# Last stage of a fused conv/attention kernel: image 3 first, own banks, taps of two pairs in turns

## Chip, cores and metric

The kernel runs on one core of one Trainium2 chip. The metric is the time of one execution on the device in microseconds (us), median of several runs. Inside a trace times are counted from the start of the profiled span.

## What is computed

The input x has 4 images of 128 channels and 16 x 16 points (N = 256 points). Four residual layers follow each other; each starts with a group norm `_gn` (32 groups of 4 channels, statistics per image):

```python
x = x + attention(_gn(x))        # L0: q, k, v projections, softmax(q k^T / sqrt(C)) v, output projection
x = x + binary_conv(_gn(x))      # L1: batch norm, sign, grouped 3x3 conv of signs, batch norm, residual, PReLU
x = x + depthwise_block(_gn(x))  # L2: 3x3 depthwise conv, norm, relu, prune, 1x1 conv, norm, relu, prune
x = x + linear_attention(_gn(x)) # L3: q,k,v; softmax(k) over points; context = k v^T per head; out = w_out (context q) + b
```

The change lies mostly in L2 and L3. In L2 a channel of the depthwise output is zeroed if its largest value is under 4.0, and a channel of the block's output if its largest value is under 0.001. L3 needs the group norm of x after L2 (x3), for each image by itself.

## The kernel before

Everything stays in on-chip memory; all loops are unrolled and the order of the work on every engine is a list of calls written out by hand. The engines are TensorE (PE), VectorE (DVE), ScalarE (ACT), GpSimd (POOL) and SyncE (SP, the output DMAs). Each takes its list strictly from top to bottom; a wait at one call holds back all calls below it on that engine. Semaphores tie the lists together.

**Depthwise convolution (L2), TensorE.** The images are worked in two pairs p = 0, 1. For each of the 9 taps, `depthwise(p, tap)` (L1499) issues 8 small fp32 matmuls: 4 blocks of 32 channels times 2 images, each on its own 32 x 32 tile of the array (`tile_of`, L1493). Each fp32 matmul is two passes in the trace, so a tap is 16 matmul records and 16 weight loads. The 8 tiles that pair 0 uses and the 8 that pair 1 uses are different ones, and the results lie in different banks. `less_mean(p)` (L1532) adds the norm's mean term as a tenth, equal step, and its end (`dw_mm`) lets ACT and DVE start on the pair: `relu1` (L702), `prune1_max` (L1160), `prune1_weights` (L1169). `group_means2(p)` (L1515) is a full-array matmul of statistics. `pointwise(p)` (L1552) is the 1 x 1 convolution; it waits for `relu1` and the pruned weights, first of r = 1, then of r = 0.

**x3 and its norm.** DVE reads the pointwise result: `prune2_max` (L1176), `prune2_floor` (L1182), `x3_out(b)` (L1190, gives x3 and its sum). ACT takes the squares, `square_sum3(b)` (L686). POOL corrects the sum, `x3_sum_less_floor(b)` (L492). `group_means3(b)` (L1544, matmul L1549) on TensorE waits for both. Then DVE `group_out(3, b)` and `group_var(3, b)` (L853, L860), POOL `gn_root` (L369) and DVE `norm3(b)` (L869; image 1 on POOL, L506) give the normalised image t3.

**L3, for each image b.** TensorE: `project_k3` (L1577), `project_v3` (L1596), `project_q3` (L1587). DVE `k3_max` (L1204), ACT `softmax3` (L708, exponentials e3 and their sum). TensorE `transpose_k` (L1608), ACT `kt3_out` (L722), TensorE `context` (L1622), DVE `context_out` (L1212), TensorE `project_context` (L1632), ACT `project_out` (L729, scaled by the inverse sum, which POOL's `rinv3_out`, L513, makes), TensorE `output` (L1642), DVE `x4_out` (L1218), output DMA (L329). Before the change all `project_context` results share bank 4, and `output(b)` uses banks 6 and 2 in turn, so `output(2)` waits for `x4_out(0)` and `output(3)` for `x4_out(1)`.

`keep_warm(n)` (L1337) issues n matmuls whose result nobody reads. `rinv3_out(b)` begins with this wait:

```python
def rinv3_out(b):
    pool.wait_ge(e3_ready, b + 1)      # the exponentials of image b
```

Of the kernel before, what the change touches and what calls it, by code (L numbers as in the profile page):

```python
# [20 lines left out]
N = H * W  # L21
# [30 lines left out]
def build(nc, x, early, late, out):  # L52
# [10 lines left out]
    with ctx:  # L63
# [153 lines left out]
        pj_ps = banks[4][:, 0:C]  # L217
        y_ps = [banks[(6, 2)[b % 2]][:, 0:N] for b in range(B)]
# [114 lines left out]
        def _(pool):  # L333
# [229 lines left out]
            norm3_second(1)  # L563
            out_bias_less_floor(2)
# [3 lines left out]
            rinv3_out(0)  # L568
            mean_with_floor(2)
            gn_root(3, 2)  # L570
            mean_with_floor(3)
            rinv3_out(1)
            gn_root(3, 3)
# [3 lines left out]
        def _(act):  # L577
# [147 lines left out]
            def project_out(b):  # L725
# [3 lines left out]
                nc.scalar.activation(proj[:, b, :], pj_ps, ACT.Copy,  # L729
# [41 lines left out]
            negative_part(1)  # L771
            negative_part(2)
            square_sum2(0)
            negative_part(3)
            square_sum2(1)
# [9 lines left out]
            softmax3(0)  # L785
            q3_out(0)
            kt3_out(0)
            square_sum3(2)
            square_sum3(3)
            softmax3(1)  # L790
            v3_out(1)
            kt3_out(1)
            project_out(0)
            q3_out(1)
            softmax3(2)
            v3_out(2)
            kt3_out(2)
            softmax3(3)
            project_out(1)
            v3_out(3)  # L800
            kt3_out(3)
            project_out(2)
            q3_out(3)
            project_out(3)
        @block.vector
        def _(dve):
# [217 lines left out]
            def bn1_mean():  # L1024
                dve.wait_ge(rstd_ready[1], B)
# [3 lines left out]
                settle("bn1_e2")  # L1029
                step(nc.vector.tensor_scalar(bn1_e2[:, 1:2], bn1_e2[:, 0:1], EPS, None, ALU.add),  # L1030
                     "bn1_e2_eps")

            def bn1_var():
                settle("bn1_e2_eps")
                mean = bn_mv[:, 0, 0:1]
# [227 lines left out]
            norm1(2)  # L1263
            bn1_mean()
            bn1_var()
            norm1(3)
# [14 lines left out]
            h1_out(2)  # L1281
            x2_first_out(0)
            x2_first_out(1)
            h1_out(3)
# [15 lines left out]
            x3_out(1)  # L1300
            group_out(3, 0)
            group_var(3, 0)
            prune1_max(1, 1)
            group_out(3, 1)
            norm3(0)
            group_var(3, 1)
            prune1_weights(1, 1)
            prune1_max(1, 0)
            prune1_weights(1, 0)
            k3_max(0)  # L1310
# [5 lines left out]
            x3_out(3)  # L1316
            k3_max(1)
            group_out(3, 2)
            group_var(3, 2)
            context_out(0)  # L1320
            group_out(3, 3)
            group_var(3, 3)
            norm3(2)
            norm3(3)
            k3_max(2)
            context_out(1)
            k3_max(3)
            q3_out(2)
            x4_out(0)
            context_out(2)  # L1330
            context_out(3)
            x4_out(1)
            x4_out(2)
            x4_out(3)
# [453 lines left out]
```

## Time and profile before

| what | value |
|---|---|
| median of 3 runs (lowest to highest) | 70.4 us (70.36 to 70.52) |
| the profiled execution's own time | 70.48 us |
| its span | 68.8 us |
| PE busy | 59.6 us (87%) |
| DVE / ACT / POOL busy | 43.2 / 33.7 / 32.8 us |
| granted TensorE clock | full in the whole span |

The span begins with the first and ends with the last recorded work; 1.7 us of the profiled time lie outside it. A busy share is an average over stages with different limits; which wait ends last must be read stage by stage.

### The profile page before, as it was taken

What the parts mean: (1) busy time and instruction counts of PE and PEld (TensorE: products, weight loads), DVE (VectorE), ACT (ScalarE), POOL (GpSimd) and SP (SyncE); (2) the same over time, 40 slices, a digit from 0 to 9 for tenths busy, and PEclk for the clock granted to TensorE, in tenths of its full rate; (3) what the DMA queues carried; (4) which work ended last, traced back from release to release, by engine and by line L of the source; (5) the groups of instructions that cost most, each with busy time, mean ns of one, the idle gap of its engine ahead of it and who ended that gap; (6) DMA issues with size and microseconds to landing.
All of it is one profiled execution on the core that took longest, in us unless ns stands there. A gap on an engine that the chain in (4) does not pass through costs nothing.

```text
span 68.8 us, 1882 instructions
## 1 busy us (share of the span) xinstructions
PE 59.6 (87%) x666; PEld 47.1 (68%) x666; DVE 43.2 (63%) x168; ACT 33.7 (49%) x106; POOL 32.8 (48%) x98
## 2 busy tenths in 40 slices
PE   3994998999999979299988999999999978999530
PEld 2772777989999858188855676665676966997310
DVE  3959868577755988864569900939395975443520
ACT  5202686496987220573177820603464775481500
POOL 5805385889997454970030062074657396330000
PEclk9999999999999999999999999999999999999999
DMA  0597220000000000000000000000000000002222
GB/s 0 147 404 233 41 39 2 0 0 0 0 5 0 14 0 0 0 5 10 0 0 0 0 0 10 0 10 0 0 0 0 10 0 5 0 0 76 74 79 76
DMA packets 2777, 2.13 MB, mean 31 GB/s; under 512 B 976, under 2 KB 2512, under 8 KB 2768
## 3 DMA queue, kind: packets, MB, share of 16 engines
q1 hardware_dynamic: 2768, 2.01, 9.6%
q8 instruction: 5, 0.08, 0.5%
q14 instruction: 4, 0.03, 0.2%
HBM read 1.49 MB, written 0.52 MB: 29 GB/s over the span
## 4 chain that ended last, share of the span: by engine, by line
PE 66%; DVE 10%; issue 10%; DMA 5%; POOL 2%; ACT 1%; SPq 1%
PE bank L1511 13%; PE bank L1466 6%; PE bank L1424 5%; DMA x<-in_x 5%; PE bank L1453 4%; PE bank L1577 3%; PE bank L1642 3%; PE bank L1563 3%; PE bank L1400 3%; PE bank L1596 3%; PE bank L1435 3%; PE bank L1587 3%; PE bank L1622 3%; PE bank L1393 3%; PE bank L1412 2%
## 5 line engine op out<-in xcount | busy, mean ns | idle before, releaser
L1340 PE MATMUL bank<-warm 128*128 128x256 bf16 x70 | 10.5, 304 | 1.2 <-POOL warm L353 1.2
L369 POOL TENSOR_TENSOR gn_rstd<-gn_var_eps,minus_half 128x1 f32<-128x1 f32 (+2 forms) x12 | 7.3, 610 | 5.6 <-DVE gn_var_eps L860 4.1
L1511 PE MATMUL bank<-x,dw_diag 32*32 32x256 f32 x288 | 9.2, 377 | 0.3 <-DVE x L1123 0.3
L1340 PEld LDWEIGHTS bank<-warm 128*128 128x128 bf16 x70 | 7.6, 114 | 2.6 <-POOL warm L353 1.1
L1511 PEld LDWEIGHTS bank<-x,dw_diag 32*32 32x32 f32 x288 | 5.2, 103 | 2.3 <-issue 0.9
L1466 PE MATMUL bank<-signs,conv_blocks 128*128 128x256 bf16 x36 | 4.3, 276 | 1.3 <-ACT signs L647 1.3
L1466 PEld LDWEIGHTS bank<-signs,conv_blocks 128*128 128x128 bf16 x36 | 3.4, 97 | 2.2 <-issue 1.6
L473 POOL TENSOR_TENSOR mean_diag<-ident_tile,gn_group 128x64 f32<-128x64 f32 x2 | 0.6, 294 | 8.1 <-DVE gn_group L1143 8.1
L1424 PE MATMUL bank<-k,q 128*128 128x256 f32 x16 | 4.2, 386 | 0.2 <-DVE k L953 0.2
L702 ACT ACTIVATE h<-bank,l_shift,dw_scale 128x256 f32<-128x256 f32 x4 | 2.3, 565 | 4.2 <-PE bank L1539 3.9
L1160 DVE TENSOR_SCALAR_CACHE_REDUCE h_linear<-bank,dw_scale 128x256 f32<-128x256 f32 x4 | 1.9, 480 | 3.8 <-PE bank L1539 3.8
L1453 PE MATMUL bank<-vt,probT 128*128 128x128 f32 x32 | 4.3, 277 | 0.0
L620 ACT ACTIVATE prob<-bank,nmax 128x256 f32<-128x256 f32 x8 | 3.7, 472 | 0.9 <-DVE nmax L958 0.9
L1453 PEld LDWEIGHTS bank<-vt,probT 128*128 128x128 f32 x32 | 4.0, 192 | 0.0
L647 ACT ACTIVATE signs<-res,bn_shift,bn_scale 128x256 bf16<-128x256 f32 x4 | 2.1, 592 | 3.7 <-issue 3.7
L686 ACT ACTIVATE squares<-x,floor 128x256 f32<-128x256 f32 x4 | 2.0, 508 | 3.5 <-DVE x L1190 3.4
L958 DVE TENSOR_REDUCE nmax<-bank 128x2 f32<-128x512 f32 x4 | 2.8, 692 | 1.4 <-PE bank L1424 1.3
L513 POOL TENSOR_TENSOR rinv<-sum,minus_one 128x1 f32<-128x1 f32 x4 | 2.2, 554 | 2.7 <-ACT e L708 2.7
L1642 PE MATMUL bank<-q,proj 128*128 128x256 f32 x8 | 2.5, 398 | 1.0 <-issue 1.0
L403 POOL TENSOR_TENSOR conv_blocks<-conv_sign,conv_mask 128x128 bf16<-128x128 bf16 x9 | 3.4, 401 | 0.1
L369 POOL TENSOR_TENSOR bn_rstd<-bn_var_eps,minus_half 128x1 f32<-128x1 f32 x2 | 1.2, 604 | 4.4 <-DVE bn_var_eps L1080 3.6
L1424 PEld LDWEIGHTS bank<-k,q 128*128 128x128 f32 x16 | 2.9, 196 | 0.6 <-issue 0.4
(197 smaller groups left out, 156.2 us busy)
## 6 DMA issues: line engine op xcount, KB each, us to landing
out<-x SPq DMA_DIRECT2D x4, 128.0 KB, 1.7
late_params<-in_late SPq DMA_DIRECT2D x1, 404.5 KB, 4.5
x<-in_x SPq DMA_DIRECT2D x1, 384.0 KB, 3.6
early_params<-in_early SPq DMA_DIRECT2D x1, 258.0 KB, 3.8
x<-in_x SPq DMA_DIRECT2D x1, 128.0 KB, 2.1
pw_weights<-in_late SPq DMA_DIRECT2D x2, 64.0 KB, 3.5
pw_weights<-in_late SPq DMA_DIRECT2D x4, 32.0 KB, 1.8
l_params<-in_late SPq DMA_DIRECT2D x4, 2.2 KB, 1.7
```

The source lines that it names most:

```text
L369: return nc.gpsimd.tensor_tensor(out_ap, in_ap, minus_half[:, 0:n], ALU.pow)
L403: ins = nc.gpsimd.tensor_tensor(conv_w[:, tap, :].rearrange("p (g o) -> p g o", o=CONV_GROUP), conv_sign[:, tap, :].unsqueeze(1).to_broadc ...
L513: nc.gpsimd.tensor_tensor(rinv3[:, b:b + 1], sum3[:, b:b + 1], minus_one[:, :], ALU.pow).then_inc(rinv3_ready, 1)
L620: nc.scalar.activation(prob[:, b, par, :], s_ps[b % 2][:, par * N:(par + 1) * N], ACT.Exp, bias=nmax[:, b, par:par + 1], accum_out=psum_ro ...
L702: nc.scalar.activation(h2[:, p, r, :], dw_ps[p][r], ACT.Relu, bias=l2_shift[:, 3 * p + r:3 * p + r + 1], scale=dw_scale[:, p, r:r + 1]).th ...
L958: nc.vector.tensor_reduce(nmax[:, b, :], s_ps[b % 2][:, :].rearrange("p (a c) -> p a c", a=2), X_AXIS, ALU.max, negate=True).then_inc(nmax ...
L1340: nc.tensor.matmul(bank[:, 0:N], warm[:, 0:C], warm[:, :], start=True, stop=True)
L1424: ins = nc.tensor.matmul(s_ps[b % 2][:, par * N:(par + 1) * N], q[:, b, par:N:2], k[:, b, :], start=True, stop=True)
L1453: ins = nc.tensor.matmul(o_ps[b][:, par * C:(par + 1) * C], probT[:, b, j, par, :], vt[:, b, j, :], start=(j == 0), stop=(j == 1))
L1466: ins = nc.tensor.matmul(conv_ps[b], conv_w[:, tap, :], signs[:, b, dy:dy + H, dx:dx + W], start=(tap == 0), stop=(tap == TAPS - 1))
L1511: nc.tensor.matmul(tile_of(p, i, r), dw_diag[of, tap, :], xs[2][of, 2 * p + i, dy:dy + H, dx:dx + W], start=(tap == 0), stop=False)
L1642: nc.tensor.matmul(y_ps[b], proj[:, b, :], q3[:, b, :], start=True, stop=True).then_inc(y3_mm, 1)
```

## The change

Three kinds of edits. (1) `project_context(3)` gets bank 5, `output(2)` bank 1 and `output(3)` bank 3, with the waits that go with them; `q3_out(3)` moves from ACT to DVE. (2) Taps 6, 7, 8 of pair 0 and 0, 1, 2 of pair 1 are issued in turns. (3) The calls of the last stage, and a few of the batch norms, stand in another order on all four engines. On POOL `rinv3_out(0)` now stands ahead of `out_bias_less_floor(2)` and `x3_sum_less_floor(2)`; on ACT `softmax3(0)` stands behind `square_sum3(3)` and `kt3_out(0)` ahead of `softmax3(1)`; on DVE `k3_max(0)` stands behind `x3_out(3)`, and `context_out(0)` between `norm3(2)` and `norm3(3)`; on TensorE `transpose_k(0)`, `context(0)` and `transpose_k(1)` stand behind `group_means3(3)` and ahead of `project_k3(2)`. `keep_warm(4)` comes in ahead of `group_means3(1)`.

```diff
--- before.py
+++ after.py
@@ -214,8 +214,8 @@
         k3_ps = [banks[(6, 2)[b % 2]][:, 0:N] for b in range(B)]
         vt_ps = banks[5][:, 0:N]
         kt_ps = banks[1][:, 0:N]
-        pj_ps = banks[4][:, 0:C]
-        y_ps = [banks[(6, 2)[b % 2]][:, 0:N] for b in range(B)]
+        pj_ps = [banks[i][:, 0:C] for i in (4, 4, 4, 5)]
+        y_ps = [banks[i][:, 0:N] for i in (6, 2, 1, 3)]
         gn_ps = banks[7]
         cx_ps = [banks[(3, 7)[b % 2]][:, 0:C] for b in range(B)]
 
@@ -561,16 +561,16 @@
             mean_with_floor(1)
             gn_root(3, 1)
             norm3_second(1)
+            rinv3_out(0)
             out_bias_less_floor(2)
             x3_sum_less_floor(2)
             out_bias_less_floor(3)
             x3_sum_less_floor(3)
-            rinv3_out(0)
             mean_with_floor(2)
             gn_root(3, 2)
             mean_with_floor(3)
+            gn_root(3, 3)
             rinv3_out(1)
-            gn_root(3, 3)
             rinv3_out(2)
             rinv3_out(3)
         @block.scalar
@@ -726,7 +726,7 @@
 
                 act.wait_ge(pj_mm, b + 1)
                 act.wait_ge(rinv3_ready, b + 1)
-                nc.scalar.activation(proj[:, b, :], pj_ps, ACT.Copy,
+                nc.scalar.activation(proj[:, b, :], pj_ps[b], ACT.Copy,
                                      scale=rinv3[:, b:b + 1]).then_inc(pj_ready, 1)
 
             act.wait_ge(setup_done, 1)
@@ -769,10 +769,10 @@
             bn2_diagonal()
             negative_part(0)
             negative_part(1)
+            square_sum2(0)
             negative_part(2)
-            square_sum2(0)
+            square_sum2(1)
             negative_part(3)
-            square_sum2(1)
             square_sum2(2)
             square_sum2(3)
             relu1(0, 0)
@@ -782,25 +782,24 @@
             relu1(1, 0)
             relu1(1, 1)
             v3_out(0)
-            softmax3(0)
             q3_out(0)
-            kt3_out(0)
             square_sum3(2)
             square_sum3(3)
+            softmax3(0)
+            kt3_out(0)
             softmax3(1)
             v3_out(1)
             kt3_out(1)
-            project_out(0)
             q3_out(1)
             softmax3(2)
             v3_out(2)
+            softmax3(3)
+            project_out(0)
             kt3_out(2)
-            softmax3(3)
-            project_out(1)
             v3_out(3)
             kt3_out(3)
+            project_out(1)
             project_out(2)
-            q3_out(3)
             project_out(3)
         @block.vector
         def _(dve):
@@ -1022,16 +1021,17 @@
                     op0=ALU.mult, op1=ALU.mult, accum_out=bn1_e2[:, 0:1]), "bn1_e2")
 
             def bn1_mean():
+                settle("bn1_e2")
+                step(nc.vector.tensor_scalar(bn1_e2[:, 1:2], bn1_e2[:, 0:1], EPS, None, ALU.add),
+                     "bn1_e2_eps")
                 dve.wait_ge(rstd_ready[1], B)
                 step(nc.vector.scalar_tensor_tensor(
                     out=bn1_tmp[:, 1, :], in0=bn1_dev[:, :], scalar=1.0 / B, in1=rstd[:, 1, :],
                     op0=ALU.mult, op1=ALU.mult, accum_out=bn_mv[:, 0, 0:1]), "bn_mv", 0)
-                settle("bn1_e2")
-                step(nc.vector.tensor_scalar(bn1_e2[:, 1:2], bn1_e2[:, 0:1], EPS, None, ALU.add),
-                     "bn1_e2_eps")
 
             def bn1_var():
                 settle("bn1_e2_eps")
+                settle("bn_mv", 0)
                 mean = bn_mv[:, 0, 0:1]
                 nc.vector.scalar_tensor_tensor(
                     out=bn_ve[:, 0:1], in0=mean, scalar=mean, in1=bn1_e2[:, 1:2], op0=ALU.mult,
@@ -1260,9 +1260,9 @@
             group_out(1, 3)
             group_var(1, 3)
             bn1_mean_sq()
-            norm1(2)
             bn1_mean()
             bn1_var()
+            norm1(2)
             norm1(3)
             bn_scale_out(0)
             bn_shift_out(0)
@@ -1278,9 +1278,9 @@
             h1_minus_out(0)
             h1_minus_out(1)
             bn2_minus_shift()
-            h1_out(2)
             x2_first_out(0)
             x2_first_out(1)
+            h1_out(2)
             h1_out(3)
             x1_h1_out(2)
             x1_h1_out(3)
@@ -1298,37 +1298,38 @@
             x3_out(0)
             prune2_floor(1)
             x3_out(1)
+            prune1_max(1, 1)
             group_out(3, 0)
             group_var(3, 0)
-            prune1_max(1, 1)
-            group_out(3, 1)
-            norm3(0)
-            group_var(3, 1)
             prune1_weights(1, 1)
             prune1_max(1, 0)
+            group_out(3, 1)
+            group_var(3, 1)
             prune1_weights(1, 0)
-            k3_max(0)
+            norm3(0)
             prune2_max(2)
             prune2_floor(2)
             prune2_max(3)
             x3_out(2)
             prune2_floor(3)
             x3_out(3)
+            k3_max(0)
             k3_max(1)
             group_out(3, 2)
             group_var(3, 2)
-            context_out(0)
             group_out(3, 3)
             group_var(3, 3)
             norm3(2)
+            context_out(0)
             norm3(3)
             k3_max(2)
+            k3_max(3)
             context_out(1)
-            k3_max(3)
             q3_out(2)
             x4_out(0)
             context_out(2)
             context_out(3)
+            q3_out(3)
             x4_out(1)
             x4_out(2)
             x4_out(3)
@@ -1627,9 +1628,11 @@
                 pe.wait_ge(cx_ready, b + 1)
                 if b == 0:
                     pe.wait_ge(x3_ready, B)
+                elif b < 3:
+                    pe.wait_ge(pj_ready, b)
                 else:
-                    pe.wait_ge(pj_ready, b)
-                nc.tensor.matmul(pj_ps, ctxT[:, b, :], lp[:, LC["woutT"]],
+                    pe.wait_ge(vt3_ready, B)
+                nc.tensor.matmul(pj_ps[b], ctxT[:, b, :], lp[:, LC["woutT"]],
                                  start=True, stop=True).then_inc(pj_mm, 1)
 
             def output(b):
@@ -1637,8 +1640,10 @@
                 pe.wait_ge(pj_ready, b + 1)
                 if b < 2:
                     pe.wait_ge(e3_ready, b + 3)
+                elif b == 2:
+                    pe.wait_ge(kt3_ready, B)
                 else:
-                    pe.wait_ge(x4_ready, b - 1)
+                    pe.wait_ge(cx_ready, 3)
                 nc.tensor.matmul(y_ps[b], proj[:, b, :], q3[:, b, :],
                                  start=True, stop=True).then_inc(y3_mm, 1)
 
@@ -1702,54 +1707,55 @@
             depthwise(0, 4)
             depthwise(0, 5)
             depthwise(0, 6)
+            depthwise(1, 0)
             depthwise(0, 7)
+            depthwise(1, 1)
             depthwise(0, 8)
+            depthwise(1, 2)
             less_mean(0)
-            depthwise(1, 0)
             group_means2(1)
-            depthwise(1, 1)
-            depthwise(1, 2)
-            pointwise(0)
             depthwise(1, 3)
             depthwise(1, 4)
+            pointwise(0)
             depthwise(1, 5)
             depthwise(1, 6)
             depthwise(1, 7)
-            group_means3(0)
             depthwise(1, 8)
             less_mean(1)
+            group_means3(0)
+            keep_warm(4, gap_warm_ps)
             group_means3(1)
             keep_warm(7, gap_warm_ps)
+            pointwise(1)
             project_v3(0)
             project_k3(0)
-            pointwise(1)
             project_q3(0)
-            transpose_k(0)
             project_k3(1)
             project_v3(1)
             project_q3(1)
-            context(0)
             group_means3(2)
             group_means3(3)
-            project_context(0)
+            transpose_k(0)
+            context(0)
             transpose_k(1)
             project_k3(2)
             project_v3(2)
             project_k3(3)
             context(1)
+            project_context(0)
+            transpose_k(2)
             project_q3(2)
-            transpose_k(2)
+            project_v3(3)
+            transpose_k(3)
+            project_context(1)
             output(0)
-            project_v3(3)
-            project_context(1)
-            transpose_k(3)
             context(2)
+            context(3)
             project_q3(3)
+            project_context(2)
+            project_context(3)
             output(1)
-            context(3)
-            project_context(2)
             output(2)
-            project_context(3)
             output(3)
```

## Rows read from the trace of the kernel before

**Rows 1.** The page's chain that ended last, share of the span by engine.
```profile
PE 66%; DVE 10%; issue 10%; DMA 5%; POOL 2%; ACT 1%; SPq 1%
```

**Rows 2.** Timeline, batch norm and first taps: start us, length us, engine, line, operation, count.
```profile
26.18 0.41 DVE L869 TENSOR_SCALAR res<-x,gn_group,gn_rstd 128x256 f32<-128x256 f32 x1
...
36.90 0.47 DVE L1123 SCALAR_TENSOR_TENSOR x<-h_neg,one_minus_a,bank 128x256 f32<-128x256 f32 x1
...
37.53 1.53 PE L1511 MATMUL bank<-x,dw_diag 32*32 32x256 f32 x48 [0.33 <-DVE x L1123]
```

**Rows 3.** Timeline of TensorE (PE matmuls, PEld weight loads), end of pair 0's taps to pointwise.
```profile
41.82 0.64 PE L1511 MATMUL bank<-x,dw_diag 32*32 32x256 f32 x16
...
42.25 0.42 PE L1539 MATMUL bank<-valid_sum,mean_diag 32*32 32x256 f32 x8
...
42.44 0.23 PEld L1511 LDWEIGHTS bank<-x,dw_diag 32*32 32x32 f32 x14
42.44 0.42 PE L1511 MATMUL bank<-x,dw_diag 32*32 32x256 f32 x3
42.47 0.38 PE L1539 MATMUL bank<-valid_sum,mean_diag 32*32 32x256 f32 x2
...
43.09 0.38 PE L1521 MATMUL bank<-gn_mean_sq,group_sum 128*128 128x2 f32 x2
...
44.76 1.14 PE L1563 MATMUL bank<-h,pw_kept 64*128 64x256 f32 x8
```

**Rows 4.** Timeline, from the last step of pair 1 to the last x3.
```profile
48.91 0.64 PE L1539 MATMUL bank<-valid_sum,mean_diag 32*32 32x256 f32 x16
...
51.70 1.13 PE L1563 MATMUL bank<-h,pw_kept 64*128 64x256 f32 x8
...
54.44 0.48 DVE L1190 SCALAR_TENSOR_TENSOR x<-bank,floor,x 128x256 f32<-128x256 f32 x1
```

**Rows 5.** Timeline, norm of x3 and start of the last stage's second half.
```profile
52.26 0.47 ACT L708 ACTIVATE e<-bank,nmax 128x256 f32<-128x256 f32 x1 [0.51 <-DVE nmax L1204]
52.64 0.19 ACT L708 ACTIVATION_READ_ACCUMULATOR e<-bank,nmax 128x1 f32 x1
...
54.31 0.51 ACT L686 ACTIVATE squares<-x,floor 128x256 f32<-128x256 f32 x1 [0.16 <-DVE x L1190]
54.38 0.27 POOL L492 TENSOR_SCALAR gn_mean_sq<-floor,x_sum 128x1 f32<-128x1 f32 x1 [0.56 <-DVE x L1190]
...
55.27 0.56 POOL L513 TENSOR_TENSOR rinv<-sum,minus_one 128x1 f32<-128x1 f32 x1
55.27 0.28 PE L1549 MATMUL bank<-gn_mean_sq,group_sum 128*128 128x2 f32 x2
...
56.61 0.38 PE L1608 MATMUL bank<-ident,e 128*128 128x128 f32 x2
...
57.02 0.38 ACT L722 ACTIVATE kt<-bank 128x256 f32<-128x256 f32 x1 [0.72 <-PE bank L1608]
...
57.16 0.70 PE L1577 MATMUL bank<-t,late_params 128*128 128x256 f32 x2 [0.17 <-DVE t L869]
```

**Rows 6.** Timeline, the end of the kernel.
```profile
62.71 0.61 PE L1622 MATMUL bank<-kt,vt 128*128 128x128 f32 x4
...
66.15 0.48 DVE L1218 SCALAR_TENSOR_TENSOR x<-bank,out_bias,x 128x256 f32<-128x256 f32 x1 [0.91 <-PE bank L1642]
```

**Rows 7.** The chain of waits in order of time: start us, length us, what.
```profile
59.48 0.43 PE bank L1587 x2
59.91 0.22 PE bank L1608 x2
...
63.54 0.50 issue
```

**Rows 8.** Timeline of TensorE's warm matmuls (L1340), at the start and later.
```profile
1.15 3.17 PE L1340 MATMUL bank<-warm 128*128 128x256 bf16 x14 [1.15 <-POOL warm L353]
...
49.72 0.92 PE L1340 MATMUL bank<-warm 128*128 128x256 bf16 x7
```

## The prediction

> **What bounds the kernel now.** I read the page's chain first: two thirds of what ended last is TensorE [rows 1]. So the order of TensorE's list matters most, but a third of the chain is short work of other engines that TensorE waits for. The timeline then shows where. From the first tap (37.53) to the second pointwise product (51.70) TensorE is nearly always occupied [rows 2 to 4]. Then it waits for the norm of x3: the statistics matmul of image 2 runs at 55.27, and the first k projection that needs its norm at 57.16 [rows 5]. From there to the last context product at 62.71 it is full again [rows 5, 6], and the last microseconds are turn-taking between TensorE, ACT and DVE, with 0.50 us "issue" ahead of an output product [rows 7]. A change of about 0.2%, or 0.14 us, is the least that a measurement of this kernel can tell from none.
>
> I go along the timeline; "at" means the start of an operation on the clock of the trace of before, and every shift is against it.
>
> **Step 1, batch norm and first taps.** `norm1(2)`, 0.41 us, no longer stands ahead of the batch-norm variance [rows 2]. The short products in front still take their time, so I take -0.17 us, between 0 and -0.41. `h1_out(2)` no longer stands ahead of the two `x2_first_out`; the second (36.90) also waits for the linear matmuls, so I take another -0.10 (0 to -0.40). The delayed `h1_out(2)` makes `square_sum2(1)` no later, since ACT had `negative_part(2)` ahead of it before too. First tap: 37.53 becomes 37.26 [rows 2].
>
> **Step 2, taps in turns.** Tap 8 of pair 0 starts at 41.82 and `less_mean(0)`, the next step on the same tiles, at 42.25: 0.43 us a step, while one step lasts 0.64 us from first start to last end [rows 3]. A tile takes a new pass each 0.22 us and each step has two, so a single pair is bound by its tiles. Pair 1 uses the other tiles. The one place where both are in flight is `less_mean(0)` with tap 0 of pair 1: the tap's first matmuls start at 42.44, 0.19 us behind 42.25, and ahead of the second pass of `less_mean(0)` at 42.47. So the pairs do overlap. But 14 of the tap's 16 weight loads begin only at 42.44, when tap 8, two steps back, is finishing (41.82 + 0.64 = 42.46) [rows 3]. I read this as a limit: a step can be taken up only when the step two before it retires. In turns that means 0.64 us for each two steps, where tiles alone would need 0.43 and no overlap 0.86.
> Pair 0's tap 6 was at 40.96 (41.82 - 2 x 0.43) and is now at 40.69. Three turns of 0.64 put `less_mean(0)` at 40.69 + 1.91 = 42.60, +0.35 against 42.25; its passes are stretched too, so its end and `group_means2(1)` come at 43.24, +0.15 against 43.09, with two more taps of pair 1 done. Between `group_means2(1)` and `pointwise(0)` stand two taps as before, 1.67 us (43.09 to 44.76) [rows 3]: `pointwise(0)` at 44.91, +0.15. The pruned weights, +0.4, are needed only for its second half, and are in time.
>
> **Step 3, to the second pointwise.** After `pointwise(0)` (1.07 us to the next step, its 1.14 [rows 3] less the overlap at its end) stand four taps instead of six and no statistics matmul among them: 44.91 + 1.07 + 4 x 0.44 = 47.73 for `less_mean(1)`, -1.18 against 48.91 [rows 4]. The warm matmuls began 0.81 us after it (49.72), seven lasting 0.92 us [rows 8]. The four new ones cost 0.5 us of TensorE at most and are covered: `group_means3(1)` waits till about 49.2 for DVE, which has `prune1_max(1, 1)` ahead of `group_out(3, 0)`. Then about 0.24 us for it (an estimate, a third of those 0.81) and 0.92 for seven warm ones give `pointwise(1)` at 50.41, -1.29 against 51.70 [rows 4]. It no longer waits behind `project_v3(0)` and `project_k3(0)`. The last x3 starts at 53.15 instead of 54.44 and ends at 53.64 [rows 4]. So far this is a gain of 1.29 us.
>
> **Step 4, what POOL waits for.** Here it is lost. `x3_sum_less_floor(2)` ran at 54.38 as soon as x3 was there, and `rinv3_out(0)` at 55.27 behind it [rows 5]. Now it stands behind `rinv3_out(0)`, which waits for `softmax3(0)`, which on ACT stands behind `square_sum3(3)`, which waits for the last x3. ACT squares images 2 and 3 in 0.51 us each, from 53.47 to 54.49. `softmax3(0)` takes 0.57 us to its read sum (52.26 to 52.64 + 0.19): 55.06. Then POOL: 0.07 us to notice, 0.56 for the reciprocal, 0.17 for a bias, 0.27 for the sum [rows 5]: 56.13. `group_means3(2)` at 56.23, +0.96 against 55.27 [rows 5]. The queue alone costs 1.29 + 0.96 = 2.25 us. Late with it: both x3 sums, both norms, and on TensorE all that stands behind.
>
> **Step 5, to the k projection of image 2.** Before, it came when its norm did. Now `transpose_k(0)`, `context(0)` and `transpose_k(1)` stand ahead. `group_means3(3)` is 0.7 us behind `group_means3(2)` (56.93), and 0.21 us later comes `transpose_k(0)` (57.14). Its copy on ACT starts some 0.43 us later and lasts 0.38 (56.61, 57.02) [rows 5]: done at 57.96. Only then ACT comes to `softmax3(1)`, 0.57 us, 58.53, for which `transpose_k(1)` waits: 58.63. One transpose is 0.22 us of TensorE [rows 7]: `project_k3(2)` at 58.85, +1.69 against 57.16 [rows 5]. Its norm, at about 58.15, is no longer what it waits for.
>
> **Step 6, to the last context product.** Before, 5.55 us (57.16 to 62.71) [rows 5, 6]. Now eight steps of 0.43 to 0.44 us (k, v of 2, k of 3, context 1, q of 2, v of 3, output 0, context 2), four of 0.22 (two `project_context`, two transposes) [rows 7], and about 0.27 us ahead of `transpose_k(3)`, since ACT has `softmax3(3)` and `project_out(0)` ahead of `kt3_out(2)`: 3.48 + 0.88 + 0.27 = 4.63 us, `context(3)` at 63.48. That is -0.92.
>
> **Step 7, the end.** Before, 3.44 us from `context(3)` to the last `x4_out` (62.71 to 66.15) [rows 6]. Now TensorE has `context(3)`, `project_q3(3)`, two `project_context`, and outputs 1, 2, 3 one behind the other: 0.44 + 0.43 + 2 x 0.22 + 2 x 0.44 = 2.19 to the start of `output(3)`, and some 0.66 to DVE, 2.85 us. The own banks are what allows this; the projection of image 3 is ready 0.1 us ahead of its turn. -0.59. `q3_out(3)` on DVE has its place in the wait for output 1: nothing; if DVE were late there, 0.4 us. The last three DMAs come 0.43 us apart instead of 1.3; nothing is taken for this (up to +0.1).
>
> **Sum.** +1.69 - 0.92 - 0.59 = +0.18 us at the last `x4_out`. The profiled execution took 70.48 us, so 70.66; the median is 0.08 lower, so 70.6.
>
> **Rivals.**
> - *A, the pairs overlap fully* (tiles alone, 0.43 us a turn). Then `less_mean(0)` is at 41.98, the product behind it 0.69 us earlier than in my sum, and all that follows TensorE with it: 69.9. For it: the tiles are separate. Against: the 14 late loads [rows 3]. The sum is 0.18 us over before and there are three turns, so at 0.58 us a turn it breaks even, and below 0.53 it is faster by over 0.2%. This case ends on the other side. 0.2.
> - *B, no overlap* (a turn costs 0.86). `group_means2(1)` comes 0.61 us later than in my sum: 71.2. Against: 42.44 before 42.47 [rows 3]. 0.08.
> - *C, the clock.* From about 54.2 to 58.2 TensorE has four tiny statistics matmuls and two or three small steps, a far emptier stretch than any before, where the full clock was kept. The first 14 warm matmuls took 3.17 us, 0.23 each, against 0.13 later [rows 8]: that is the price of the lower level, 1.2 instead of 2.4 GHz. If the clock falls near 58, some 3 us of TensorE's steps take nearly twice their time, of which waits hide half: 72.1. 0.12.
> - *D, the waits of step 4 and 5 are shorter*, as when the copy and softmax chain of images 0 and 1 is hidden and `project_k3(2)` comes at its norm, 58.15: 69.9. 0.1. That the order has no such queueing at all is excluded by the lists.
>
> On B: the Trainium skill, "TensorE: Matmul & The Clock Gate", section on packing small matmuls, says that matmuls are "strict FIFO, no reordering" in start and end. By that rule the pairs would hold each other up as in B, at 71.2. The records at 42.44 and 42.47 speak against it, and the measurement decides. On C: the same page's part on the clock gate says that the clock is gated down when TensorE has been idle; by it the time would be C's. No run here shows it inside a kernel.
>
> **How the numbers follow.** My sum 0.5, A 0.2, B 0.08, C 0.12, D 0.1. The sum's own range, from steps 1 and 5 to 7, is 70.2 to 71.1, a fifth of it within 0.2% of 70.4 or just below. The range must take in A and D on one side and B on the other, and leaves out C: 69.6 to 71.4. Faster: A, D and 0.02 = 0.32. Same: 0.18. Slower: the rest of the sum, B and C = 0.50.
>
> **What would show it.** Right: `less_mean(0)` about 0.64 us per turn behind tap 6 of pair 0; `pointwise(1)` at about 50.4; POOL's reciprocal of image 0 ahead of `x3_sum_less_floor(2)`, waiting for ACT; TensorE empty from about 54.2 to 56.2; outputs 1 to 3 back to back. Wrong: turns of 0.45 us or 0.86 us; `group_means3(2)` ahead of 55.5; a granted clock under full between 55 and 62; `project_k3(2)` ahead of 58.2.

## The result, and the profile of the changed kernel

The changed kernel is slower: ratio to before 1.044, 95% interval 1.038 to 1.050. Its four runs took 73.35, 73.65, 74.95 and 75.19 us, against 70.36 to 70.52 us for three of before and 71.99 for a fourth. Run again (below) it gave 71.78 to 73.55 us; the three lowest of those six have a ratio of 1.020 (1.017 to 1.022). The forecast was 70.6 us in a range to 71.4: the direction was right, the size was not, and the time lies outside the range.

TensorE has two clock levels, 2.4 and 1.2 GHz; the granted clock is the share of the full one that the profile reports, over a whole run or a stretch of it. A run of this kernel can hold a stretch at the lower level, early or late, so the mean granted clock is given where it matters. Single runs of all these kernels, of before too, can come out 1.5 us or more longer, and each ratio is of the runs near the lowest alone.

The timeline of the changed kernel (lines after 1340 are numbered one higher, after 1635 five higher), at the places of [rows 2 to 6]; start us, length us, engine, line, operation, count, and in brackets what ended the idle time before it:

```profile
38.88 1.53 PE L1512 MATMUL bank<-x,dw_diag 32*32 32x256 f32 x48 [0.31 <-DVE x L1123]
...
44.83 0.38 PE L1522 MATMUL bank<-gn_mean_sq,group_sum 128*128 128x2 f32 x2
...
46.51 1.14 PE L1564 MATMUL bank<-h,pw_kept 64*128 64x256 f32 x8
...
51.87 1.16 PE L1564 MATMUL bank<-h,pw_kept 64*128 64x256 f32 x8
...
54.62 0.48 DVE L1190 SCALAR_TENSOR_TENSOR x<-bank,floor,x 128x256 f32<-128x256 f32 x1
...
55.35 0.49 ACT L686 ACTIVATE squares<-x,floor 128x256 f32<-128x256 f32 x1
...
55.85 0.45 ACT L708 ACTIVATE e<-bank,nmax 128x256 f32<-128x256 f32 x1
...
56.47 0.56 POOL L513 TENSOR_TENSOR rinv<-sum,minus_one 128x1 f32<-128x1 f32 x1 [2.46 <-ACT e L708]
...
57.17 0.27 POOL L492 TENSOR_SCALAR gn_mean_sq<-floor,x_sum 128x1 f32<-128x1 f32 x1
...
57.53 0.35 PE L1550 MATMUL bank<-gn_mean_sq,group_sum 128*128 128x2 f32 x2 [1.68 <-issue]
...
58.90 0.38 ACT L722 ACTIVATE kt<-bank 128x256 f32<-128x256 f32 x1 [2.51 <-PE bank L1609]
...
59.34 1.22 PE L1623 MATMUL bank<-kt,vt 128*128 128x128 f32 x4 [0.47 <-ACT kt L722]
...
60.78 1.06 PE L1578 MATMUL bank<-t,late_params 128*128 128x256 f32 x2
...
65.57 1.05 PE L1623 MATMUL bank<-kt,vt 128*128 128x128 f32 x8
```

The queue of step 4 stands there as it was worked out: POOL idle for 2.46 us until the exponentials of image 0, the reciprocal, and behind it the sum of x3 (57.17) that TensorE waits for. What the sum did not hold is seen in lengths: a context product of 0.61 us [rows 6] (0.71 where it follows a wait, as in the run with the gap filled below) takes 1.22 us at 59.34, a k projection 1.06 at 60.78. The granted clock says why. Stretches of the changed kernel; columns are the stretch in us, its length, then busy us and count of TensorE, its weight loads, DVE, ACT and POOL, then PEclk (1.00 is 2.4 GHz, 0.50 is 1.2 GHz), DMA share and GB/s:

```profile
7.00:11.00 4.00, 3.79 (x15) 3.27 (x16) 2.81 (x15) 2.18 (x8) 2.03 (x5) 0.58 0.22 36
...
54.00:56.00 2.00, 1.85 (x11) 1.35 (x9) 1.74 (x8) 1.52 (x7) 0.01 (x1) 1.00 0.00 0
56.00:58.00 2.00, 0.35 (x2) 0.30 (x2) 0.08 (x1) 0.39 (x2) 1.34 (x5) 1.00 0.00 0
58.00:60.00 2.00, 1.30 (x7) 1.09 (x8) 1.06 (x5) 1.10 (x4) 1.81 (x5) 0.72 0.00 0
60.00:62.00 2.00, 2.00 (x9) 1.82 (x9) 0.74 (x3) 0.67 (x3) 0.36 (x1) 0.50 0.02 4
62.00:64.00 2.00, 2.00 (x16) 1.92 (x15) 1.01 (x3) 1.35 (x6) 0.55 (x1) 0.93 0.00 0
```

TensorE is nearly empty from 56 to 58. Between 58 and 60 the clock goes to half, stays there through 60 to 62, and comes back after 62. And there is a second low stretch, between 7 and 11 us, where no engine's list was changed.

The chain of waits of the changed kernel at the gap and at the end (start us, length us, what):

```profile
54.96 0.99 ACT squares L686 x4
55.95 1.58 issue
57.53 0.37 PE bank L1550 x2
...
68.92 0.48 DVE x L1218
```

The last `x4_out` starts at 68.92, 2.77 us behind the 66.15 of before. Of this 1.35 us are there at the first tap (38.88 against 37.53 [rows 2]) and 1.42 come behind it (68.92 - 38.88 = 30.04, against 66.15 - 37.53 = 28.62).

### The profile page after: what moved, and what is told of

The parts are those of the page before. It is cut to its first block, busy times and chain, and to the rows that moved or that the text cites. A ratio compares the mean times of both kernels' runs of the same rounds, so it can differ in the third digit from the quotient of the medians.

```text
span 71.6 us, 1891 instructions
## 1 busy us (share of the span) xinstructions
PE 61.3 (86%) x670; PEld 49.4 (69%) x670; DVE 43.6 (61%) x169; ACT 32.9 (46%) x105; POOL 32.8 (46%) x98
## 2 busy tenths in 40 slices
DMA packets 2777, 2.13 MB, mean 30 GB/s; under 512 B 976, under 2 KB 2512, under 8 KB 2768
## 4 chain that ended last, share of the span: by engine, by line
PE 65%; issue 10%; DVE 9%; DMA 5%; ACT 4%; POOL 2%; SPq 1%
PE bank L1512 11%; PE bank L1467 6%; DMA x<-in_x 5%; PE bank L1425 5%; PE bank L1454 4%; PE bank L1623 4%; PE bank L1394 3%; PE bank L1564 3%; PE bank L1401 3%; PE bank L1436 3%; PE bank L1647 3%; PE bank L1597 3%; PE bank L1413 3%; PE bank L1578 2%; PE bank L1550 2%
## 5 line engine op out<-in xcount | busy, mean ns | idle before, releaser
L1341 PE MATMUL bank<-warm 128*128 128x256 bf16 x74 | 11.0, 300 | 1.2 <-POOL warm L353 1.2
L1512 PE MATMUL bank<-x,dw_diag 32*32 32x256 f32 x288 | 8.1, 379 | 0.3 <-DVE x L1123 0.3
L1550 PEld LDWEIGHTS bank<-gn_mean_sq,group_sum 128*128 128x128 f32 x8 | 1.2, 188 | 3.2 <-issue 2.5
L1623 PE MATMUL bank<-kt,vt 128*128 128x128 f32 x16 | 2.9, 321 | 0.5 <-ACT kt L722 0.5
```

The source lines that it names most:

```text
L1341: nc.tensor.matmul(bank[:, 0:N], warm[:, 0:C], warm[:, :], start=True, stop=True)
L1512: nc.tensor.matmul(tile_of(p, i, r), dw_diag[of, tap, :], xs[2][of, 2 * p + i, dy:dy + H, dx:dx + W], start=(tap == 0), stop=False)
L1550: nc.tensor.matmul(gn_ps[:, 0:2], group_sum[:, :], mv[:, 3, b, 0:3:2], start=True, stop=True).then_inc(group_ready[3], 1)
L1623: ins = nc.tensor.matmul(cx_ps[b], vt3[:, b, j, :], kt3[:, b, j, :], start=(j == 0), stop=(j == 1))
```

## The experiments

Each kernel ran on the same chip as the runs of before that its ratio is against, whose median was 70.56 to 70.59 us. Four chips were used: one for the changed kernel again, the gap filled, the reciprocal back and the turns alone; the others for the rest. Kernels on different chips are best compared by their ratios.

**The changed kernel again** (no edit).

> The changed kernel once more, for the spread of single runs and of their mean clock. Theory Q+C (the queue on POOL empties TensorE for about 2 us, and the clock falls behind it): every run has a mean clock under 1, the late stretch at the lower level costs about 1.0 us, and runs differ by whether the clock also falls near 7 us (1.6 us more), where the change touches nothing: about 71.7 without, 73.3 with. Rival R (everything of the +2.9 us is the new order itself): all runs at 73 or more whatever their clock.

Measured: 71.78, 71.86 and 71.94 us at a mean clock of 0.976, and 73.17, 73.17 and 73.55 us at 0.952; the ratio of 1.020 is of the first three, and the median of all six is 72.55. Neither these six, nor the four of the result, nor six more below had a mean clock over 0.977, so the late fall is part of this order and not chance. The profiled run of 73.55 us had no early fall (its clock was full from 7 to 11 us) but a late one twice as long:

```profile
56.00:58.00 2.00, 1.21 (x6) 0.79 (x6) 1.00 (x5) 0.16 (x1) 1.63 (x7) 0.80 0.00 0
58.00:60.00 2.00, 1.72 (x7) 1.73 (x8) 0.59 (x3) 0.99 (x5) 1.08 (x2) 0.50 0.00 0
60.00:62.00 2.00, 2.00 (x8) 1.73 (x8) 0.57 (x2) 1.34 (x5) 0.08 (x1) 0.50 0.02 4
62.00:64.00 2.00, 2.00 (x11) 1.91 (x10) 0.72 (x2) 0.88 (x4) 0.84 (x2) 0.50 0.00 0
64.00:66.00 2.00, 2.00 (x16) 1.90 (x16) 0.46 (x2) 1.47 (x5) 0.17 (x1) 0.99 0.00 0
```

So 0.952 can be one early and one late stretch (the first profile) or a late one of double length. The expectation named only the first. The last three `x4_out` begin 30.58 us behind the first tap here (68.17 - 37.59), where the first profile had 29.09 (67.97 - 38.88).

**Warm matmuls in the gap.** The queue stays; only the emptiness goes.

```diff
             project_q3(1)
+            pe.wait_ge(x3_ready, 3)
+            keep_warm(18, banks[3])
             group_means3(2)
```

> The changed kernel with 18 warm matmuls in the empty stretch of TensorE ahead of group_means3(2) (18 x 0.109 = 2.0 us), in a bank that is free there; the queue on POOL stays. Theory Q+C: group_means3(2) not more than 0.1 us later, no low clock behind it, 1.0 us less than the changed kernel: about 70.6 without and 72.2 with a fall near 7 us. Rival (the late loss is not the clock's): no gain.

Measured: 70.51 us median, ratio 1.000 (0.998 to 1.002); one of the twelve runs took 72.19, at a mean clock of 1.000. The timeline of TensorE in it:

```profile
54.22 2.13 PE L1341 MATMUL bank<-warm 128*128 128x256 bf16 x18
56.19 0.28 PE L1550 MATMUL bank<-gn_mean_sq,group_sum 128*128 128x2 f32 x2
...
57.91 0.71 PE L1623 MATMUL bank<-kt,vt 128*128 128x128 f32 x4 [0.47 <-ACT kt L722]
58.71 0.60 PE L1578 MATMUL bank<-t,late_params 128*128 128x256 f32 x2
```

No product is stretched and the clock is 1.00 in every stretch from 50 to 66 us. Useless work in an otherwise idle engine took 1.3 us off the 71.8. This shows that the late loss is the clock's. It also shows the order's own cost with the clock full: nothing, 70.5 against 70.4 to 70.6. That is the number that the sum of the prediction was for.

**The reciprocal back behind the sums of x3.**

```diff
             norm3_second(1)
-            rinv3_out(0)
             out_bias_less_floor(2)
             x3_sum_less_floor(2)
             out_bias_less_floor(3)
             x3_sum_less_floor(3)
+            rinv3_out(0)
```

> Only rinv3_out(0) goes back behind x3_sum_less_floor(3) on POOL. Theory Q+C: the statistics matmul of image 2 follows project_q3(1) at once, project_k3(2) comes 1.9 us earlier, no low clock late in the kernel: 1.9 + 1.0 us less than the changed kernel, about 68.7 in a run whose clock stays full, 70.3 in one whose clock falls near 7 us. Rival R (the low clock or other stalls are not due to this queue): 0.5 us less at most, and the clock still falls late.

Measured: 68.54, 68.55, 68.55 and 68.61 us, and the profiled run with 70.54; median 68.55, ratio 0.973 (0.971 to 0.975). One line on POOL is worth 3.3 us against the 71.8 of the changed kernel: 2.0 of queue (70.51 to 68.55) and 1.3 of clock. The timeline of this kernel (its first tap at 39.29, since the profiled run had the early fall):

```profile
54.97 0.26 POOL L492 TENSOR_SCALAR gn_mean_sq<-floor,x_sum 128x1 f32<-128x1 f32 x1 [0.38 <-DVE x L1190]
...
56.10 0.28 PE L1550 MATMUL bank<-gn_mean_sq,group_sum 128*128 128x2 f32 x2
...
56.89 0.56 POOL L513 TENSOR_TENSOR rinv<-sum,minus_one 128x1 f32<-128x1 f32 x1 [0.99 <-ACT e L708]
...
58.63 0.68 PE L1578 MATMUL bank<-t,late_params 128*128 128x256 f32 x2
```

`project_k3(2)` comes 19.34 us behind the first tap, where the kernel with warm matmuls had 21.30 (58.71 - 37.41).

**The same POOL order in the kernel of before.**

```diff
             norm3_second(1)
+            rinv3_out(0)
             out_bias_less_floor(2)
             x3_sum_less_floor(2)
             out_bias_less_floor(3)
             x3_sum_less_floor(3)
-            rinv3_out(0)
```

> The kernel of before with rinv3_out(0) ahead of out_bias_less_floor(2) on POOL, nothing else. Theory Q (the move costs only because softmax3(0) was put behind the squares of images 2 and 3): the reciprocal finds its sum at 52.8 and is done ahead of the floor of image 2, no change, 70.4. Rival (the POOL order costs by itself): 1 us or more.

Measured: 70.48 us, ratio 1.000 (0.997 to 1.003). On its POOL timeline the reciprocal runs at 52.97 without a wait:

```profile
52.97 0.56 POOL L513 TENSOR_TENSOR rinv<-sum,minus_one 128x1 f32<-128x1 f32 x1
...
54.43 0.27 POOL L492 TENSOR_SCALAR gn_mean_sq<-floor,x_sum 128x1 f32<-128x1 f32 x1 [0.57 <-DVE x L1190]
```

The move is harmless by itself. In the changed kernel POOL waits for the exponentials ([2.46 <-ACT e L708] above), which come late because `softmax3(0)` stands behind the squares of images 2 and 3; it costs only together with that.

**The turns alone, in the kernel of before.**

```diff
             depthwise(0, 6)
+            depthwise(1, 0)
             depthwise(0, 7)
+            depthwise(1, 1)
             depthwise(0, 8)
+            depthwise(1, 2)
             less_mean(0)
-            depthwise(1, 0)
             group_means2(1)
-            depthwise(1, 1)
-            depthwise(1, 2)
-            pointwise(0)
             depthwise(1, 3)
             depthwise(1, 4)
+            pointwise(0)
```

> The kernel of before with the taps in turns alone. Theory W (a step is taken up only when the step two before it has retired, 0.64 us for two): less_mean(0) about 0.6 us later than before, two taps fewer behind pointwise(0), but group_means3(0) then waits for its statistics, 0.4 us late: 70.8, +0.3 us. Rival A (full overlap, 0.43 us a turn): less_mean(0) not later, 70.0 or less. Rival B (no overlap): less_mean(0) 1.3 us later, 71.3.

Measured: 70.79 us, ratio 1.004 (1.003 to 1.006). Its TensorE timeline:

```profile
43.50 0.38 PE L1521 MATMUL bank<-gn_mean_sq,group_sum 128*128 128x2 f32 x2
...
45.17 1.14 PE L1563 MATMUL bank<-h,pw_kept 64*128 64x256 f32 x8
46.23 1.52 PE L1511 MATMUL bank<-x,dw_diag 32*32 32x256 f32 x48
48.44 0.38 PE L1549 MATMUL bank<-gn_mean_sq,group_sum 128*128 128x2 f32 x2 [0.68 <-ACT squares L686]
```

`group_means2(1)` is 0.41 us later than in [rows 3], with two more taps done, which alone would cost 0.87. The taps saved behind `pointwise(0)` end in 0.68 us of waiting for ACT's squares: the gain is hidden, since x3 of pair 0 comes later.

**The turns taken out again, with the queue mended** (the reverse of that edit, in the kernel with the reciprocal moved back).

> e1_rinv_back (the queue on POOL mended), with the taps in the order of before. Theory W (turns save TensorE 0.87 us of taps and cost 0.15 us at pointwise(0)): less_mean(1) and all behind it 0.7 us later, 69.25 against 68.55. Rival (the turns' gain is covered, as it was in e3_turns_alone): 68.5 to 68.7.

Measured: 69.18 us (one of six runs 70.64), ratio 0.981 (0.979 to 0.983), against 68.55 and 0.973. So the turns do gain 0.6 us where `group_means3(0)` no longer stands between the last taps: the second pointwise comes 13.46 us behind the first tap (50.83 - 37.37) instead of 12.99.

**Own banks and the end that goes with them, in the kernel of before** (banks and waits as in the change, and):

```diff
             context(2)
-            project_q3(3)
-            output(1)
             context(3)
+            project_q3(3)
             project_context(2)
-            output(2)
             project_context(3)
+            output(1)
+            output(2)
             output(3)
```

> The kernel of before with the own banks and the end that they allow (context 2 and 3, project_q3(3), both projections, outputs 1 to 3; q3_out(3) on DVE), nothing else. By steps 6 and 7: context(3) waits for kt3_out(3) till 62.25, then 2.85 us to the last x4_out, 65.1 against 66.15: 69.4. Rival (the banks give nothing, since waits on ACT end last there): 70.2 to 70.4.

Measured: 69.71 us (69.50 to 69.88), ratio 0.989 (0.986 to 0.991). Two lines of its timeline:

```profile
62.06 0.71 PE L1622 MATMUL bank<-kt,vt 128*128 128x128 f32 x4 [0.23 <-ACT kt L722]
...
64.13 1.43 DVE L1217 SCALAR_TENSOR_TENSOR x<-bank,out_bias,x 128x256 f32<-128x256 f32 x3 [0.45 <-PE bank L1646]
```

The last context product waits for its copy and the three `x4_out` follow each other, the last about 0.95 us behind 64.13. That start is the 65.1 that was expected; the median is 0.3 us over the expected time, for which I have no cause.

**The batch-norm and x2 order alone, in the kernel of before** (DVE: `bn1_mean`, `bn1_var` ahead of `norm1(2)`, `x2_first_out` ahead of `h1_out(2)`; ACT: `square_sum2(0)` and `(1)` one place up).

> The kernel of before with the order of the batch norm and of the first x2 results alone (DVE and ACT). By step 1: the first tap 0.27 us earlier, 70.15. Rival (these waits end elsewhere, on POOL or on the linear matmuls): first tap not more than 0.1 us earlier, 70.35 to 70.45.

Measured: median 70.63, but four of twelve runs at 71.9 to 72.0 and one at 73.4; the other seven give a ratio of 0.998 (0.995 to 1.000), hardly to be told from none. Its timeline from the last batch-norm product to the second x2 result:

```profile
27.69 0.16 DVE L1020 SCALAR_TENSOR_TENSOR bn_products<-bn_mean_sq,bn_inv_var 128x4 f32<-128x4 f32 x1
...
28.24 0.22 DVE L1037 SCALAR_TENSOR_TENSOR bn_var_eps<-bn_mean_var,bn_e 128x1 f32<-128x1 f32 x1
...
37.10 1.13 PE L1484 MATMUL bank<-conv_neg,bn_scale_diag 128*128 128x256 f32 x4 [0.27 <-ACT bn_scale_diag L661]
...
38.34 0.48 DVE L1124 SCALAR_TENSOR_TENSOR x<-h_neg,one_minus_a,bank 128x256 f32<-128x256 f32 x1
```

The same in the kernel of before, as far as [rows 2] do not have it:

```profile
26.09 0.16 DVE L1020 SCALAR_TENSOR_TENSOR bn_products<-bn_mean_sq,bn_inv_var 128x4 f32<-128x4 f32 x1
...
26.77 0.22 DVE L1036 SCALAR_TENSOR_TENSOR bn_var_eps<-bn_mean_var,bn_e 128x1 f32<-128x1 f32 x1
...
35.63 1.13 PE L1483 MATMUL bank<-conv_neg,bn_scale_diag 128*128 128x256 f32 x4 [0.27 <-ACT bn_scale_diag L661]
```

The profiled run took 71.94 us, with long matmuls in the first 8 us (five warm ones take 1.23 us where before they took 0.83), so only distances count. The variance starts 0.55 us behind the last product (28.24 - 27.69), where before it was 0.68 (26.77 against 26.09): -0.13, of the -0.17 that I took. The second x2 result starts 1.24 us behind the linear matmuls (38.34 - 37.10), where before it was 1.27 (36.90 [rows 2] against 35.63): -0.03, of the -0.10 that I took. Together -0.16 us, which the ratio of 0.998 (-0.17 us) agrees with, though its interval takes in a ratio of 1. The expectation's 70.15 was too low.

**A better order.**

```diff
-            rinv3_out(0)
             mean_with_floor(2)
             gn_root(3, 2)
             mean_with_floor(3)
             gn_root(3, 3)
+            rinv3_out(0)
...
             context(0)
-            transpose_k(1)
             project_k3(2)
+            transpose_k(1)
```

> e1_rinv_back, with rinv3_out(0) behind gn_root(3, 3), and project_k3(2) ahead of transpose_k(1). In e1 TensorE stands idle 0.1 to 0.4 us ahead of transpose_k(1) and project_k3(2), whose norm waited for the reciprocal. Theory: project_k3(2) follows context(0) at once, 0.3 us earlier: 68.2. Rival (transpose_k(1) and its copy, now later, become the wait): 68.5 or more.

Measured: 68.45, 68.50 and 68.53 us, and three runs of 70.30 to 70.46; ratio of the first three 0.971 (0.969 to 0.974), against 0.973 without the two moves. The 0.3 us did not come; 0.05 to 0.1 did, inside the intervals. The expectation's rival fits: counted from the first tap, `project_k3(2)` is 0.25 us earlier (19.09 against 19.34), `transpose_k(1)` 0.44 later (19.53 against 19.09), and the last three `x4_out` begin 0.09 earlier (25.78 against 25.87).

**More warm matmuls in the first 7 us.** Two of the three runs of 70.3 to 70.5 us had a mean clock of 0.975 (the third 0.999), and the profiled one of these two has the early fall:

```profile
3.50:7.00 3.50, 2.02 (x15) 1.32 (x13) 2.35 (x11) 0.20 (x1) 0.95 (x3) 1.00 0.90 301
7.00:11.00 4.00, 3.83 (x14) 3.16 (x14) 2.67 (x15) 1.93 (x8) 2.00 (x4) 0.57 0.21 35
```

What differs from profile to profile there is how long TensorE waits for the input parameters: they land at different times, and the five warm matmuls ahead take 0.71 to 1.23 us. TensorE's first product that needs them, in the changed kernel and in before:

```profile
5.76 0.49 PE L1369 MATMUL bank<-early_params 128*128 128x128 f32 x2 [0.72 <-DMA early_params<-in_early]
...
5.53 0.49 PE L1368 MATMUL bank<-early_params 128*128 128x128 f32 x2 [0.30 <-DMA early_params<-in_early]
```

The three profiles with the early fall (the changed kernel, the reciprocal moved back, the better order) waited 0.72, 0.99 and 0.91 us there; the eight without it and without added early matmuls waited 0.39 us or less. The edit fills that stretch:

```diff
-            keep_warm(5)
+            keep_warm(8)
             fold_weights()
-            keep_warm(2)
+            keep_warm(8)
```

In the kernel with the reciprocal moved back:

> e1_rinv_back with 9 more warm matmuls in the first 7 us (8 instead of 5, 8 instead of 2), where TensorE waits for parameters and the first norm. Theory: the runs at 70.3 to 70.5 of e1 and e7 are a fall of the clock behind this sparse stretch; with it filled no run is over 69, median 68.6. Rival (the early fall has another cause): one run in three or four still 1.8 us longer.

In the better order:

> e7_better with the 9 early warm matmuls of e9. Theory (the early fall follows the sparse stretch in the first 7 us): no run near 70.3, where e7 had three of six; median 68.5 to 68.7, all runs within 0.4 us. Rival (chance, the early fall has another cause): a third to a half of the runs at 70.3.

In the changed kernel:

> The changed kernel with the 9 early warm matmuls, the late gap left as it is. Theory: each run has the late fall and none the early one: 71.8 to 71.9 or, where the late one lasts two steps, 73.2; mean clock 0.95 to 0.98 in every run, none at 70.5. Rival (the early and the late fall are one cause): with the early one gone the late one goes too, 70.5.

Measured: 68.73 us (five runs, 68.52 to 68.85), 68.64 us (six, 68.56 to 69.10) and 72.38 us (72.19 to 72.45, one 73.49; mean clock 0.976 in five, 0.952 in one). In the first two no run of eleven had a fall (mean clock 0.995 or more), where the kernels they come from had three of eleven at 0.975. That alone is not proof: they ran on other chips than those kernels, and six more kernels with the same first 11 us and nothing added (the gap filled, the turns alone, the turns taken out, the POOL order, the banks and the early order alone) had no mean clock under 0.985 in 55 runs. From 3.5 to 7 us TensorE is full there:

```profile
3.50:7.00 3.50, 3.50 (x25) 2.89 (x24) 2.70 (x14) 0.54 (x3) 1.35 (x4) 1.00 0.83 276
7.00:11.00 4.00, 3.87 (x23) 3.28 (x23) 3.04 (x13) 2.82 (x11) 1.61 (x3) 1.00 0.23 35
```

The third keeps its late fall in every run, so the late one does not hang on the early stretch. Its 72.38 is 0.5 us over what was expected. The profiled run shows 0.18 of it: the clock falls earlier (0.64 from 58 to 60), when TensorE has more to do, and the last three `x4_out` begin 29.27 us behind the first tap (66.79 - 37.52) instead of 29.09; the rest is open. The extra matmuls cost the other two 0.1 to 0.2 us in the median (68.55 to 68.73, 68.50 to 68.64), and nothing to 0.2 us by the ratios (0.973 to 0.973, 0.971 to 0.974).

## Why the prediction was wrong, step by step

Places counted from the first tap, so that the early stretch falls out. "Expected" is from the steps; the third column is the changed kernel, the last the one with warm matmuls in the gap, whose clock stays full.

| place | expected | changed kernel | gap filled |
|---|---|---|---|
| `group_means2(1)` (step 2) | 5.98 | 5.95 | 5.96 |
| `pointwise(0)` | 7.65 | 7.63 | 7.63 |
| `pointwise(1)` (step 3) | 13.15 | 12.99 | 12.99 |
| last x3 | 15.89 | 15.74 | 15.74 |
| `group_means3(2)` (step 4) | 18.97 | 18.65 | 18.78 |
| `project_k3(2)` (step 5) | 21.59 | 21.90 | 21.30 |
| last `x4_out` (step 7) | 29.07 | 30.04 | 28.71 |

**Steps 2 to 7 were right** in mechanism, each within 0.2 us, and together 0.36 us too long. The turn limit of 0.64 us for two steps holds: rival A would have had `group_means2(1)` at 5.3, rival B at 6.6. On B the Trainium skill, "TensorE: Matmul & The Clock Gate", section on packing small matmuls, has matmuls start and end in strict order. By the records of [rows 3], work of a later step does start ahead of the second pass of an earlier one. Nor would such an order make B by itself: matmuls that start in order can still overlap, and the measured place shows that they do. The same page of the Trainium skill, in its table of facts, gives TensorE a queue of 64. A step is 32 records, so that by this figure two steps would fill it (an estimate), which is the limit that I read from the late weight loads. No run here varied the number of records, so this reading is argued and not shown.

**Step 1** was over-sized: -0.27 us taken. Alone it gave some -0.16 us by its distances, and no difference clear of noise by its times. The first tap of the profiled runs with this order and a full clock lay at 37.2 to 37.6, around the 37.53 of before [rows 2]. This and the 0.36 us that the later steps were too long (29.07 - 28.71) partly cancel: the sum said 70.66 for a profiled execution, and the one with the clock full took 70.54. That the direction came out right is luck: the sum had +0.18 us of queue, bank and tap order, and with the clock full these make no difference (ratio 1.000). The kernel is slower by the clock alone, for which the sum had no term.

**What failed is the place of the clock in the forecast.** Steps 5 and 6 have transposes, context products and projections at their full-clock lengths, so the clock stands in the sum at nothing. It measured 1.3 us (71.8 against 70.5 with the gap filled), and 2.8 us where the low stretch was twice as long (30.58 against 65.17 - 37.41 = 27.76 to the last three `x4_out`). Rival C had the mechanism, the place ("from about 54.2 to 58.2", "If the clock falls near 58") and nearly the price: 1.5 us for the single fall. But it had 0.12 and was left out of the range, while it came in every one of the sixteen runs of the changed kernel, with and without the early matmuls. The sum was made at full clock through a stretch for which it had itself computed that TensorE would have nothing to do; no row of before covered such a stretch, so taking the clock as full had no row behind it either. Half or more of the chance belonged there, and a range to about 73.5. A clock under full between 55 and 62 was among the signs of being wrong, and it is the one that came.

**The early fall** was in no step. It costs some 1.3 to 2.1 us: the first tap at 38.88 to 39.29 instead of 37.2 to 37.6, and a run of 70.5 instead of 68.55 us in the mended kernel. Together with the late fall's 1.3 it accounts for the 73.35 us of the first profile. All lists there are the same before and after. That it follows a longer wait for the parameters fits the eleven profiles without added early matmuls; that filling the stretch prevents it is likely and not shown, since most kernels had no early fall without it. Whether the change makes it more frequent is open: no profile of before had it, and of the 65 runs of before beside the experiments three had a mean clock under 0.98 (0.953 to 0.965).

## What to carry to other kernels

When a new order opens a hole of a microsecond or two in TensorE's list, price the clock behind it as part of the sum, and test with warm matmuls in the hole: beside the run with the queue mended, they told queue (2.0 us) and clock (1.3 us) apart. When a call moves up on a helper engine, look for the call it waits for on the other engines' new lists; `rinv3_out(0)` cost nothing in one list and 3.3 us in the other. Before calling a reordering bad, move its single calls back: the changed kernel without that one line is 2.7% faster than before, and with 9 early warm matmuls no run was over 69.1 us (five at a median of 68.73 us, 0.973; six of the better order at 68.64, 0.974).

## What the runs showed of the hardware

- The lower clock came though TensorE was wholly idle for only 1.68 us at a time; it was busy for 1.85 us of the stretch from 54 to 56, and from 56 to 58 for the 0.35 us of one small matmul. It came when TensorE had work again, and showed in three stretches of 2 us in one profile (0.72, 0.50, 0.93) and in five in another (0.80, 0.50, 0.50, 0.50, 0.99). Behind the hole it cost 1.3 us, and 2.8 us in the second case. The Trainium skill, "TensorE: Matmul & The Clock Gate", "HAM oscillation — how this bites in real kernels", speaks of idle gaps; here the stretch was sparse and not wholly idle.
- The granted clock of the profile does not show the lower level at the start of a run. It stands at 1.00 in the first 4 us of before, yet its first 14 warm matmuls take 0.23 us each, against 0.13 later [rows 8]; that ratio is near the one of the k projection, 1.06 us at a granted clock of 0.50 and 0.60 at 1.00. So the full clock "in the whole span" of before holds behind the first 4 us, and lengths of equal matmuls are the surer sign there.
- Two tap steps on different tiles of the array overlap, but not more: the turns ran at some 0.64 us for two steps, not 0.43. This is an estimate from places: in the kernel with the gap filled, `group_means2(1)` lies 5.96 us behind the first tap, where the 0.64 of the sum gives 5.98 and 0.43 gives 5.3.
- 18 matmuls of 128 x 256 bf16, 2.13 us from first start to last end, went into a wait in which TensorE was idle for 1.68 us, and delayed little: the statistics matmul behind them came 0.13 us later than without them, counted from the first tap (18.78 and 18.65), and the clock that they kept gave back 1.3 us.
